# One core, quantised cross attention and a routed expert block: a column sum shared by four tiles, row sums moved behind a transpose, and the last product cut in two

## What is computed

```python
def fake_quant(x, scale, zp):
    q = jnp.clip(jnp.round(x / s + z), 0, 255)
    return (q - z) * s
x = x + jnp.tanh(g_xattn[0]) * jnp.matmul(fake_quant(_layernorm(x)), fake_quant(ctx_4096))
...
xt = _layernorm(x)
gate = ...                      # softmax router, 2 of 4 groups, then 2 of 16 experts, per token
for each expert: y += gate_e * ((silu(xt @ w1 + b1) * (xt @ w2 + b2)) @ w3 + b3)
z = silu(xt @ sw1 + sb1) * (xt @ sw2 + sb2) @ sw3 + sb3
x = x + jnp.tanh(g_ffn[0]) * (y + z)
```

## Time and profile before

| | |
|---|---|
| time, median of 3 runs | 316.2 us (315.91 to 316.38) |
| the profiled execution's own time | 316.27 us |
| its span in the profile | 314.3 us |
| PE busy | 293.9 us, 94% of the span |
| DVE busy | 222.8 us |
| granted TensorE clock | 0.998 of full speed |

### The profile page before, as it was taken

One profiled execution on the slowest core, in us unless ns is written; L12 is line 12 of the kernel. 1 busy time (PEld: TensorE's weight loads), 2 busy tenths in 40 slices (PEclk: granted clock), 3 DMA queues, 4 the chain that ended last, 5 costly groups with the idle time before them and its releaser, 6 DMA issues.

```text
span 314.3 us, 4647 instructions
## 1 busy us (share of the span) xinstructions
PE 293.9 (94%) x1868; PEld 149.4 (48%) x1868; DVE 222.8 (71%) x392; ACT 114.9 (37%) x130; POOL 24.3 (8%) x34
## 2 busy tenths in 40 slices
PE   0388999999999999999999999999999999999993
PEld 0224598954544445544444444444444444444441
DVE  2898987895898953685475988868784769659110
ACT  2998558769653540210343305302015040100000
POOL 2010200000002210000000011100101110000000
PEclk9999999999999999999999999999999999999999
DMA  7999970248710753000897600000000000600302
GB/s 277 413 325 346 301 219 6 82 136 168 230 60 0 136 106 95 2 2 0 250 306 250 229 39 2 0 0 0 2 0 0 2 1 0 255 15 1 133 33 104
DMA packets 35700, 35.56 MB, mean 113 GB/s; under 512 B 16068, under 2 KB 30428, under 8 KB 35548
## 3 DMA queue, kind: packets, MB, share of 16 engines
q1 hardware_dynamic: 35664, 35.23, 36.0%
q10 hardware_dynamic: 12, 0.00, 0.0%
HBM read 27.88 MB, written 4.20 MB: 102 GB/s over the span
## 4 chain that ended last, share of the span: by engine, by line
PE 83%; DVE 9%; DMA 3%; ACT 2%; SPq 1%; POOL 1%; issue 1%; DVEq 0%
PE PS L1532 26%; PE PS L1374 20%; PE PS L1565 12%; PE PS L1558 7%; PE PS L1409 7%; PE PS L1321 4%; DMA X<-in_x_dram 3%; PE PS L1390 2%; DVE stats L778 2%; PE PS L1398 2%; PE PS L1328 1%; DVE S2f L814 1%; POOL lnR L474 1%; DVE X L844 1%; DVE wrow L853 1%; DVE area L810 1%
## 5 line engine op out<-in xcount | busy, mean ns | idle before, releaser
L1374 PE MATMUL PS<-areaT,areaW 128*128 128x512 f16 x288 | 62.6, 379 | 0.0
L1374 PEld LDWEIGHTS PS<-areaT,areaW 128*128 128x128 f16 x288 | 28.0, 98 | 33.3
L1532 PE MATMUL PS<-areaT,area 128*128 128x512 f16 x192 | 42.1, 379 | 0.0
L1532 PE MATMUL PS<-areaT,areaW 128*128 128x512 f16 x192 | 42.1, 379 | 0.0
L1321 PE MATMUL PS<-area,areaQ 128*128 128x512 f16 x128 | 32.0, 400 | 1.6 <-DVE area L810 1.5
L1042 DVE SCALAR_TENSOR_TENSOR X<-PS,cf,X 128x512 f32<-128x512 f32 x22 | 15.5, 746 | 20.0 <-PE PS L1565 15.2
L1532 PEld LDWEIGHTS PS<-areaT,area 128*128 128x128 f16 x192 | 18.8, 98 | 22.7
L1532 PEld LDWEIGHTS PS<-areaT,areaW 128*128 128x128 f16 x192 | 18.8, 98 | 22.7
L778 DVE BATCH_NORM_STATS2 stats<-X 128x6 f32<-128x512 f32 x32 | 20.5, 683 | 4.5 <-DMA X<-in_x_dram 4.3
L1558 PE MATMUL PS<-SW,areaH 128*128 128x512 f16 x96 | 21.9, 379 | 0.0
L1321 PEld LDWEIGHTS PS<-area,areaQ 128*128 128x128 f16 x128 | 12.6, 102 | 17.8 <-DVE area L810 3.6
(11 more groups left out here) (187 smaller groups left out, 408.6 us busy)
## 6 DMA issues: line engine op xcount, KB each, us to landing
areaT<-in_ctx_dram SPq DMA_DIRECT2D x12, 512.0 KB, 8.1
ring<-in_L_ffn_sw_dram SPq DMA_DIRECT2D x12, 512.0 KB, 5.5
X<-in_x_dram SPq DMA_DIRECT2D x8, 512.0 KB, 7.6
ring<-in_L_ffn_ew_dram SPq DMA_DIRECT2D x16, 256.0 KB, 5.6
out_dram<-X SPq DMA_DIRECT2D x7, 512.0 KB, 2.7
ring<-in_ctx_dram SPq DMA_DIRECT2D x4, 512.0 KB, 3.8
ring<-in_L_ffn_ew_dram SPq DMA_DIRECT2D x2, 1024.0 KB, 5.0
areaQ<-gate_dram SPq DMA_DIRECT2D x1, 1024.0 KB, 6.8
```

Source lines behind the costliest of these rows:

```text
L1374: last = mm(PS[:, SU_BANK[half * SC + c] + w, lo:hi], SW[:, wp, 2 * c + w, k, :], XT[:, xp, k, tk], start=(k == 0 and n == 0), stop=(k == ...
L1532: last = mm(PS[:, EU_BANK[u] + w, :], W12S[j][:, wp, k, cs], XT[:, xp, k, b * S:(b + 1) * S], start=(k == 0 and n == 0), stop=(k == KC - 1 ...
```

## The change

Three edits, and what comes with them:

1. **Column sum of the second batch.** PE multiplies `S2` once by a matrix of ones (`column_row`, two products of 512 columns), which leaves the total of each column in all 128 rows of banks 6 and 7. ACT writes a quarter of it as f16 over `S2`; DVE replaces rows 64 to 127 by the remainder (total times a quarter minus the f16 value). A matrix `CR`, zero but for the rows 0, 32, 64 and 96 that hold the parts of the constant times 4, then adds the correction to a tile with one product for each 512 columns instead of two.
2. **First row sums.** `bias_columns()` and `row_sums(0)` move from the middle of tile 2's products to `transpose_tokens(2)`, between the turn of its high part and that of its low part; `row_terms(0)` and `shared_biases()` on DVE move behind `ln2_lo(3)`.
3. **Last product.** `P3` of the second pair of the second batch is computed as two halves of 256 columns in two banks, each with its own eviction and its own store. Stores of the last two tiles go out in smaller pieces.

```diff
+        LAST_BANK = (6, 7, 0, 1, 2, 3, 4, 5)[STEPS % 8]
...
             def turn_q1(i):
...
                     sp.wait_ge(at_done, TB)
+                    sp.wait_ge(r1_done, 1)
...
-            sp.wait_ge(y_rdy, evict_no(1, "X11f", 1))
-            store(TB + 1, slice(0, 512))
+            for pair in range(2):
+                sp.wait_ge(y_rdy, evict_no(1, "X11f", pair))
+                store(TB + pair, slice(0, 512))
             sp.wait_ge(y_rdy, evict_no(1, "X12f", 0))
-            store(TB)
+            store(TB, slice(512, D))
+            sp.wait_ge(y_first, 1)
+            store(TB + 1, slice(512, 768))
             sp.wait_ge(y_rdy, evict_no(1, "X12f", 1))
-            store(TB + 1, slice(512, D))
+            store(TB + 1, slice(768, D))
...
+            nc.gpsimd.memset(CR[:, :], 0.0).then_inc(consts, 1)
...
             small_work()
+            act.wait_ge(consts, 7)
+            act.wait_ge(c1_rdy, 1)
+            for r in range(4):
+                nc.scalar.activation(CR[32 * r:32 * r + 1, :], C1[32 * r:32 * r + 1, r % 2, :], ACT.Copy, scale=4.0)\
+                    .then_inc(cr_rdy, 1)
             su_silu_of(0)
...
             su_silu_of(3)
+            act.wait_ge(t_done, 1)
+            nc.scalar.activation(S2[:, :].rearrange("p (h n) -> p h n", h=2), PS[:, 6:8, :], ACT.Copy, scale=0.25)\
+                .then_inc(t_hi, 1)
...
+            def last_halves(x):
...
+                dve.wait_ge(dn_first, 1)
+                v.scalar_tensor_tensor(x[:, 0:256], PS[:, bank_of(1, "P3", 1), 0:256], cf[:, 11:12], x[:, 0:256], ALU.mult,
+                                       ALU.add).then_inc(y_first, 1)
+                dve.wait_ge(dn_done, STEPS)
+                v.scalar_tensor_tensor(x[:, 256:512], PS[:, LAST_BANK, 0:256], cf[:, 11:12], x[:, 256:512], ALU.mult,
+                                       ALU.add).then_inc(y_rdy, 1)
...
             attend(1)
-            row_terms(0)
-            shared_biases()
             lo_chunk("sw", 0)
...
             ln2_lo(3)
+            row_terms(0)
+            shared_biases()
             lo_chunk("sw", 4)
...
             su_gate(3)
+            dve.wait_ge(t_hi, 1)
+            half = S2[64:P, :].rearrange("p (h n) -> p h n", h=2)
+            v.scalar_tensor_tensor(half, PS[64:P, 6:8, :], 0.25, half, ALU.mult, ALU.subtract).then_inc(t_lo, 1)
             lo_chunk("sw3", 0)
...
+            def column_row():
...
+                pe.wait_ge(s2_rdy, B)
+                pe.wait_ge(su_hf, 2)
+                for h in range(2):
+                    last = mm(PS[:, 6 + h, :], onesh[:, :], S2[:, h * 512:(h + 1) * 512], start=True, stop=True)
+                last.then_inc(t_done, 1)
...
+            def add_column_row(i):
...
+                for h in range(2):
+                    last = mm(PS[:, AT_BANK[i] + h, :], CR[:, :], S2[:, h * 512:(h + 1) * 512], start=False, stop=True)
+                last.then_inc(at_done, 1)
...
+                if i == 2:
+                    bias_columns()
+                    row_sums(0)
                 pe.wait_ge(ln_lo, i + 1)
...
+            column_row()
             row_sums(1)
...
-                column_sums(i)
+                if i == TB:
+                    pe.wait_ge(t_lo, 1)
+                add_column_row(i)
...
+            def last_product():
...
+                for half, bank in enumerate((bank_of(1, "P3", 1), LAST_BANK)):
...
+                    for c in range(SC):
+                        for n, (hp, wp) in enumerate(((0, 0), (1, 0), (0, 1))):
+                            mm(o, HT[:, hp, c, P:2 * P], SW3[:, wp, c, 512 + half * 256:768 + half * 256],
+                               start=(c == 0 and n == 0), stop=False)
...
+                    last.then_inc(dn_done if half else dn_first, 1)
```

More of the change, by code:

```diff
@@ L95, in build @@
         C1 = sb("C1", [P, 2, P], F16)
+        CR = sb("CR", [P, P], F16)
         sbr = sb("sbr", [8, P], F32)
@@ L188, in build @@
         EVICTIONS = 2 * (len(EVICT[0]) + len(EVICT[1]))
-        STORES = NT + 1
+        STORES = NT + 3
         U = ring[:, :, :].rearrange("p a n -> p (a n)").rearrange("p (u n) -> p u n", n=512)
@@ L224, in build @@
         sbr_in, sb_T, sbT_rdy = sem("sbr_in"), sem("sb_T"), sem("sbT_rdy")
-        r1_done = sem("r1_done")
+        r1_done, t_done, t_hi, t_lo, cr_rdy = sem("r1_done"), sem("t_done"), sem("t_hi"), sem("t_lo"), sem("cr_rdy")
         at_done, at_read = sem("at_done"), sem("at_read")
@@ L240, in build @@
         u0_rdy = sem("u0_rdy")
+        dn_first, y_first = sem("dn_first"), sem("y_first")
         dn_done, y_rdy, y_out, rows_fin = sem("dn_done"), sem("y_rdy"), sem("y_out"), sem("rows_fin")
@@ L580, in su_silu_of @@
                 act.wait_ge(su_done, u + 1)
+                if u == 0:
+                    act.wait_ge(sbT_rdy, 2)
                 if u >= 2:
@@ L838, in shared_biases @@
                 v.tensor_scalar(sbT[:, 1, :], PS[:, 3, 8 + SC:8 + 2 * SC], UPS, None, ALU.mult).then_inc(sbT_rdy, 1)
+                dve.wait_ge(sbT_rdy, 2)
             def attend(i):
@@ L1080, in evictions @@
                     from_bank(b, "X11f", p, x11[p], "P2", x11[p], "X11u")
-                for p in range(2):
+                for p in range(2 - b):
                     from_bank(b, "X12f", p, x12[p], "P3", x12[p], "X12u")
+                if b:
+                    last_halves(x12[1])
             dve.wait_ge(x_in[0], 16)
@@ L1330, in column_sums @@
                 last.then_inc(at_done, 1)
+            def column_row():
[8 more added lines that the diff above has]
+                last.then_inc(at_done, 1)
             def row_sums(b):
-                if b == 0:
-                    pe.wait_ge(q1_rdy, TB)
-                else:
+                if b:
                     for j in range(2):
                         pe.wait_ge(q1t_in[j], 32)
-                    pe.wait_ge(at_read, TB)
+                    pe.wait_ge(r1_rdy, 1)
+                    pe.wait_ge(sbT_rdy, 2)
                 for j in range(TB):
@@ L1346, in bias_columns @@
                 pe.wait_ge(sbr_in, 32)
+                pe.wait_ge(at_read, TB)
                 nc.tensor.transpose(PS[:, 3, 8:16], sbr[:, :], idf[0:8, 0:8]).then_inc(sb_T, 1)
@@ L1447, in _ @@
                 products(2, k)
[L1448 to L1451, removed]
             column_sums(2)
-            pe.wait_ge(r1_rdy, 1)
-            pe.wait_ge(sbT_rdy, 2)
+            pe.wait_ge(q1_rdy, TB)
             for k in range(4):
@@ L1467, in _ @@
                     shared_up(0, c, w)
+            column_row()
             row_sums(1)
             pe.wait_ge(q2_rdy, 2 * KC)
-            pe.wait_ge(s2_rdy, 2)
+            pe.wait_ge(cr_rdy, 4)
             for i in range(TB, NT):
@@ L1567, in product @@
                 last.then_inc(dn_done, 1)
+            def last_product():
+                piece, blk = PRODUCT["P3"]
+                free_bank(1, "P3", 1)
+                for half, bank in enumerate((bank_of(1, "P3", 1), LAST_BANK)):
+                    if half:
+                        pe.wait_ge(y_rdy, evict_no(1, READ_LAST["P5"], 0))
+                    o, cs = PS[:, bank, 0:256], slice(half * 256, half * 256 + 256)
+                    for c in range(SC):
+                        for n, (hp, wp) in enumerate(((0, 0), (1, 0), (0, 1))):
+                            mm(o, HT[:, hp, c, P:2 * P], SW3[:, wp, c, 512 + half * 256:768 + half * 256],
+                               start=(c == 0 and n == 0), stop=False)
+                    for c in range(HC):
+                        a = pieces(1, 0, c, PIECE[piece], 1), pieces(1, 1, c, PIECE[piece], 1)
+                        for n, (hp, wp) in enumerate(((0, 0), (1, 0), (0, 1))):
+                            last = mm(o, a[hp][:, 0, 1, :], W3B[BLOCK[blk]][:, wp, c, cs], start=False,
+                                      stop=(c == HC - 1 and n == 2))
+                    last.then_inc(dn_done if half else dn_first, 1)
             pe.wait_ge(h_lo, 8)
@@ L1590, in _ @@
                 product(1, "P2", pair, (pair, 0))
-            for pair in range(2):
-                product(1, "P3", pair, (pair, 1))
+            product(1, "P3", 0, (0, 1))
+            last_product()
             n = chosen(pe)
```

1 line of the change is left out of this document (added).

## The result

The changed kernel took 313.27 us (median of 5 runs, 312.88 to 313.46), the kernel before 315.91 us (5 runs, 314.88 to 316.38). The ratio is 0.9917, with a 95% interval of 0.9899 to 0.9936: 2.64 us faster. The profiled execution took 312.88 us.

What follows compares the result with a forecast made beforehand. PE was taken to bound the kernel: 83% of the chain, without a pause from about 51 to 309 us. The terms summed as 316.27 + 0 - 1.29 + 0.1 + 0.04 - 0.5 = 314.6 us, range 312.2 to 315.2.

Steps and rivals of the forecast that it cites:

- the last store: At the kernel's end: smaller eviction and store together give -0.5 us, with an instruction fetch still holding up one queue.
- The sign: Whole kernel: forecast faster, with chance 0.88; same 0.08, slower 0.04.
- two bands: Total time: 314.2 to 315.0 us with fetch ahead of store (0.50), 312.2 to 313.0 with store ahead (0.27).
- The first rival: At the end: last store goes ahead of the fetch, tail -2.6 in place of -0.5, 312.5 us; chance 0.27.
- Column sum: Second batch on PE: 6 fewer products at 0.215 us, -1.29 us, remainder there 1.1 us early.
- The wait that follows: PE at the shared down-projection's fourth tile waits for DVE's `sd_evac(0)`: 0.1 us, bounds 0 and 0.5.
- margin of 2.8: Slack in us between `sd_evac(0)` freeing banks (116.3) and PE's fourth shared tile (119.15), forecast to shrink to 0.1.
- First row sums: PE gains 0.2 us up to tile 2's turn, then waits some 0.2 for `S2` at `column_row`: net 0.
- The blocked root: POOL's variance root near 60 us falls behind a DVE chunk: about 1.46 us instead of 0.70, DVE about 0.4 later.
- Last product: 36 products of 256 columns replace 18 of 512: 3.93 us instead of 3.88, +0.04; final eviction 0.48 us.
- the real wait: Rival: DVE's added work makes PE wait 0.5 to 1.1 us at the fourth tile, 315.1 to 315.7; chance 0.14.
- The others: Rivals: slower through `S2` lateness, 317 us, chance 0.04; or 256-column products at the price of 512, 3.9 us more.

Runs made afterwards that it cites:

- e2: The changed kernel with the third edit undone (first two edits only): 315.34 us, ratio to before 0.9988.
- e12: The kernel before with the first edit alone (column sum made once): 315.49 us, ratio to before 0.9989.
- e3: The changed kernel with its last product 512 columns wide again, keeping the two small evictions and stores: 315.52 us, ratio to before 0.9984.
- e7: The kernel before with the second edit alone (first row sums moved): 315.52 us, ratio to before 0.9994.
- e5: The kernel before, with PE reading the number of chosen experts ahead of the last two products instead of behind them: 314.44 us, ratio 0.9954.
- e4: The kernel before with its last product in two column halves in one bank, evicted and stored once as before: 314.34 us, ratio 0.9938.
- e1: The kernel before with the third edit alone (last product in halves, its evictions and stores): 314.16 us, ratio to before 0.9939.
- e6: The changed kernel, with PE waiting for its last product's end before reading the number of chosen experts and branching: 315.61 us, ratio to before 0.9990.
- e8: The changed kernel with two DVE moves: weight chunk 7's low part later, first shared down-projection eviction ahead of the last tile's low part: 315.07 us, ratio to before 0.9972.
- e9: The changed kernel with the first shared down-projection eviction moved ahead of the last tile's low part on DVE: 312.68 us, ratio to before 0.9901.
- e13: The changed kernel, on DVE: first shared down-projection eviction ahead of last tile's low part, third activation low part behind last `S2` sum: 312.73 us.

## Why the prediction was wrong

The tails of the profiled executions side by side, in us from the trace (the landing counts from the issue):

| kernel | PE's end | branch | second fetch | last store issued | landing | PE's end to span's end |
|---|---|---|---|---|---|---|
| before | 309.0 | 305.8 to 310.1 | 310.8 | 309.8 | 4.1 | 5.3 |
| e2 | 308.1 | 304.9 to 309.0 | 309.7 | 308.9 | 3.9 | 5.1 |
| e12 | 308.3 | 305.2 to 309.2 | 310.0 | 309.2 | 3.8 | 5.1 |
| e3 | 309.1 | 306.0 to 310.1 | 310.8 | 310.1 | 3.1 | 4.6 |
| e7 | 308.8 | 305.6 to 309.0 | 309.7 | 309.6 | 2.5 | 3.8 |
| e5 | 309.4 | 305.4 to 308.9 | 309.6 | 310.2 | 2.1 | 3.3 |
| e4 | 309.5 | 308.7 to 312.5 | 313.2 | 310.3 | 2.3 | 3.4 |
| e1 | 309.4 | 308.2 to 312.1 | 312.9 | 309.9 | 2.0 | 3.1 |
| after | 308.2 | 307.0 to 310.6 | 311.3 | 308.7 | 1.9 | 2.8 |
| e6 | 308.6 | 309.5 to 313.3 | 314.0 | 309.1 | 1.9 | 5.0 |

A second fetch 0.7 to 1.0 us after the issue lands among the store's packets, and the store takes 3.1 to 4.1 us. One that comes 0.6 us before the issue, or over 2 behind it, leaves it at 1.9 to 2.3, for 128 and 256 KB alike; e7, with 0.1, lies between. In the DMA records the store's first packet goes 0.83 us after its issue (in e3 it cannot be told from those of the store just ahead): in e5 the fetch is over by then (310.86 against 311.03), in e7 not quite (310.67 against 310.45). The landing of e7 had been expected near 4; its profiled execution is the shortest of twelve, 314.51 us. The fetch within the branch held up no last store: in nine of the ten it is over before the first packet, and in e6 it begins when the packets are out.

- **The step that failed** is in the last store: "If the jump asks for it, the fetch stays where it is with respect to PE's end". The jump does ask for it (e5 and e6 move it by moving nothing else), but it hangs on PE's sequencer, not on PE's end. The branch's own row in the trace of before, at 305.8, stands 3.2 us ahead of PE's end; the prediction has PE skip its loop after its end. The fetch came 1.9 us after PE's end before and 3.2 after. The term of -0.5 for eviction and store measured -2.5. The sign held; 313.27 lies in the whole range of 312.2 to 315.2, but between its two bands, 312.2 to 313.0 and 314.2 to 315.0.
- **The first rival** (store ahead of the fetch, 312.5 us) had the right outcome, a landing of 1.9 where it said near 1.8, and was nearer in time than the forecast. Its reason was the wrong one: it moved the store by 0.27 us and left the fetch where it was; in fact the fetch moved by 1.3. e3, with an earlier and smaller store but the old products, lost the gain.
- **Column sum**: -1.29 forecast and measured; the remainder was in time, and the instruction on 64 partitions took 1.23, as long as one on 128, as assumed. The wait that follows was mis-sized: 0.52 instead of 0.1. DVE came 1.64 later (94.42 against 92.78), not 1.45. The margin of 2.8 was too wide by 0.16, because it counted from the chain's 103.61, where the timeline has the product at 103.45. And 0.18 passes between the end of the eviction and PE's next product.
- **First row sums**: -0.26 at the turn, forecast -0.2. The blocked root was seen rightly: 1.61 for the 1.46 forecast, and DVE's lateness of 0.47, after the earlier start is taken off, for 0.4. The wait was 0.49 instead of 0.2; again 0.17 of it is the chain's 85.55 in place of 85.38.
- **Last product**: 36 half products came at 0.109 each, and PE's last stage grew by 0.05 for 0.04. The eviction took 0.48, as taken.
- **The rivals that cost time**: the real wait came true in kind, 0.5 us at each place, but was hidden in the total by the tail. The others did not occur.

Of the branch itself: before, its fetch landed at 308.7 and the branch ended 1.4 us later; after, 309.2 and 1.4. The Trainium skill, page "Runtime: NRT & Kernel Launch", section "Instruction fetch mechanics", says that a taken branch out of the window must have its target's page fetched first, and that further pages are prefetched in sequence. Two fetches, one within the branch and one behind it, agree with that; that the second is such a prefetch is not shown. If it is, the same section's "mostly hidden" for a page crossing does not hold for a last store, which landed after 4.1 us instead of 1.9 to 2.3.

## What to carry to other kernels

Where a program ends with a branch over code that is not run, look in the trace where that branch and its fetches lie beside the last store: one or two microseconds of lead more or less decide about 2 us, and reading the branch's operand earlier is a cheap way to move it. When work is taken from the engine that bounds the kernel, the margins of the engines behind it shrink by all that is gained, and every margin should be counted from one view, because two views may differ by the very tenths that decide. A step moved on DVE can hold SP's queue through a buffer that it sets free, as e8 showed.

## What was not expected of the hardware

PE's sequencer was through with the products 4.0 us ahead of the array for 512 columns (before, e2, e3, e7, e12) and 2.1 to 2.2 us for 256 (the changed kernel, e1, e4, e9, e13), about 19 products either way, which with a weight load each is some 38 instructions. The Trainium skill, page "TensorE: Matmul & The Clock Gate", section "Architectural detail: the array is 16× 32×32, not 1× 128×128", gives its queue a depth of 64; the lead here was shorter, and no run shows what sets it.

PE's last branch lasted 3.4 to 4.3 us in all these profiles; the branches of DVE and SP behind 300 us took 0.04 to 0.07. One instruction fetch of 16 KB could hold up a store by 2 us, because the store waits for its slowest queue: before, the fetch ran from 310.84 to 312.43, and eight packets followed from 312.41 to 313.44 when all others had gone by 311.5. Some kernels in which the two meet also scatter more, before 314.2 to 317.1 us over 26 runs, the changed kernel 312.9 to 313.5; but e3, in which they meet too, stays within 315.4 to 316.2, so that the scatter comes from it is not shown.
